# Graph attention on one core: how many pairs of gathers GpSimd keeps in flight (three or two)

## The reference

```
xn = layernorm(h)
q, k, v = xn @ wq + bq, xn @ wk + bk, xn @ wv + bv
scores = sum_d q[dst] * k[src] * scale
attn = softmax of scores over the edges (and the node itself) with the same dst
agg = segment_sum(attn * v[src], dst)
h = h + agg @ wo + bo;  h = h + gelu(layernorm(h) @ w1 + b1) @ w2 + b2
```

## Time and profile before

| | us |
|---|---|
| median of 3 timed runs | 4550.55 (4545.4 to 4551.32) |
| span of the profiled execution | 4968.2 |
| share of that span: PE, DVE, POOL, ACT busy | 76%, 74%, 66%, 45% |
| gathers (L1042): count, busy | 1760, 1775.7 |

### The profile page before, as it was taken

The page is one execution under the profiler, slowest core; times in us unless marked ns, Lnnn a source line. Parts: engine busy times, 40 slices in busy tenths (PEclk is TensorE's granted clock), DMA queues, the critical chain, the costliest instruction groups (busy, mean ns, idle before and its releaser), DMA issues. The chain is left out here.

```text
span 4968.2 us, 83663 instructions
## 1 busy us (share of the span) xinstructions
PE 3781.3 (76%) x17490; PEld 2898.5 (58%) x17491; DVE 3674.6 (74%) x10004; ACT 2245.8 (45%) x5559; POOL 3293.4 (66%) x2856
## 2 busy tenths in 40 slices
PE   2686677777777776999986677777777776888879
PEld 1344455555555555888853455555555555777766
DVE  5686688888888886666656688888888886666658
ACT  0122455555555553444410455555555563343323
POOL 2266666666666654888877666666666663888866
PEclk9698799988988998999998799999899997999989
DMA  4577666666666655777766666666666654777767
GB/s 107 176 173 172 195 184 180 184 181 180 185 175 184 178 159 127 152 160 153 160 133 132 199 181 187 183 181 181 180 180 181 183 172 97 148 143 148 143 157 222
DMA packets 683884, 831.82 MB, mean 167 GB/s; under 512 B 147301, under 2 KB 524321, under 8 KB 683589
## 3 DMA queue, kind: packets, MB, share of 16 engines
q0 software_dynamic: 261248, 480.06, 40.8%
q1 hardware_dynamic: 389483, 320.59, 22.4%
q10 hardware_dynamic: 32860, 28.05, 1.9%
HBM read 753.81 MB, written 124.16 MB: 177 GB/s over the span
## 5 line engine op out<-in xcount | busy, mean ns | idle before, releaser
L1042 POOL DMA_INDIRECT kv<-kv_scratch,src_u x1760 | 1775.7, 1009 | 955.1 <-issue 532.4
L1308 PE MATMUL sum_p<-msg,hot_s 128*128 128x273 f32 x3520 | 1132.7, 460 | 578.9 <-DVE sums L1174 452.6
L1308 PEld LDWEIGHTS sum_p<-msg,hot_s 128*128 128x128 f32 x3520 | 705.2, 215 | 893.1 <-DVE sums L1174 442.8
L1523 POOL DMA_INDIRECT sum_scratch<-ysum,dest x600 | 951.8, 1586 | 196.8 <-issue 137.8
L1296 PE MATMUL qe<-sums,hot_q 128*128 x3520 | 910.0, 404 | 99.6 <-ACT hot_q L1064 85.7
L1296 PEld LDWEIGHTS qe<-sums,hot_q 128*128 128x128 f32 x3520 | 719.5, 208 | 244.7 <-issue 115.7
L1174 DVE SCALAR_TENSOR_TENSOR sums<-sums,keep,sum_p 128x273 f32 x880 | 433.7, 493 | 463.9 <-remote 402.1
L1073 ACT ACTIVATE hot_s<-iota_f,ndrel_u 128x128 f32<-128x128 f32 x1760 | 558.7, 391 | 223.1 <-remote 173.2
L1148 DVE TENSOR_TENSOR prod<-qe,kv 128x1024 f32<-128x1024 f32 x440 | 535.6, 1217 | 64.2 <-DMA kv<-kv_scratch,src_u 35.0
L1163 DVE TENSOR_TENSOR msg<-kv,turned 128x1024 f32<-128x1024 f32 x440 | 532.6, 1210 | 7.5 <-issue 7.5
L1155 DVE TENSOR_REDUCE S<-prod 128x32 f32<-128x1024 f32 x440 | 533.8, 1213 | 0.6
(11 more groups left out here) (267 smaller groups left out, 5147.8 us busy)
## 6 DMA issues: line engine op xcount, KB each, us to landing
drow<-drel_scratch SPq DMA_DIRECT2D x220, 256.0 KB
kv<-kv_scratch,src_u POOLq DMA_INDIRECT x1760
ea<-in_edge_attr SPq DMA_DIRECT2D x52, 512.0 KB
srow<-in_src_rows SPq DMA_DIRECT2D x52, 512.0 KB
kv_scratch<-res SPq DMA_DIRECT2D x100, 256.0 KB
ea<-in_edge_attr SPq DMA_DIRECT2D x52, 384.0 KB
srow<-in_src_rows SPq DMA_DIRECT2D x52, 384.0 KB
h_scratch<-res SPq DMA_DIRECT2D x150, 128.0 KB
```

The lines of the kernel that those rows point to most:

```text
L1042: g.indirect_dma_start(out=kv[:, slot, :], out_offset=None, in_=KVd, in_offset=bass.IndirectOffsetOnAxis(ap=src_u[:, par, u:u + 1], axis=0 ...
L1308: ins = pe.matmul(sum_p[i][:, 0:XW], hot_s[:, q % 2, 2 * i + u, :], msg[:, q % 2, 2 * i + u, :], start=(u == 0), stop=(u == 1))
L1523: g.indirect_dma_start(out=sum_d[r], out_offset=bass.IndirectOffsetOnAxis(ap=dest[:, k, j:j + 1], axis=0), in_=ysum[:, k, j, :], in_offset ...
```

## The change

One constant changes. In both branches of the wait above, the pair whose landing is awaited is now j-2 in place of j-3 (counted back over the block's edge).

```diff
 HELD = 2
 PE_AT = GB - 2
-FLIGHT = 3
+FLIGHT = 2
 DVE_AT = 2
 RING = 3
```

## The result

| | us |
|---|---|
| before, median of 4 | 4549.89 (4545.4 to 4551.32) |
| changed, median of 4 | 5006.59 (5004.05 to 5016.31) |
| ratio | 1.1013, 95% interval 1.1000 to 1.1027 |

The change makes the kernel 457 us (10.1%) slower. The forecast was 4870 with a range to 4990: direction and place were right, and the loss was nearly half as large again as forecast (457 in place of 318).

What follows compares the result with a forecast made beforehand. The prediction took GpSimd's gather issue to bound the timed attention block at 21.1 us. 110 blocks x 3.1 us more, less a cover of 23, is 318 us on 4550.55: 4870 us, range 4560 to 4990.

Steps and rivals of the forecast that it cites:

- The bound and the timed block (21.1 us): In both attentions GpSimd's issue, 16 gathers at 1.31 us or 21.0 us, bounds a timed block of 21.1 us.
- its halts: GpSimd stops about 2.3 us twice a block, waiting for `sum_s`; taken to belong to the profiled execution, 310.7 us in all.
- r = 0.85 and L = 5.2: r: release to start of the waiting gather, 0.85 us; L: start of a pair's first gather to the pair's landing, 5.2.
- "The spacing of pairs is at least (L + r) / k": GpSimd's pair starts with k pairs in flight, never under 2.62 us; at FLIGHT = 2 3.02 us, 24.2 a block.
- The cover of 23 us: Gathers run 11.5 us ahead of their use; that lead is spent once in each attention, saving 23 us.
- FLIGHT = 3 "costs nothing": In the kernel before, spacing by landing is 2.02 us, below the floor of 2.62, so the wait costs nothing.
- Hidden by a short landing (1): With fewer gathers outstanding L falls to 4.4 us or less and the wait costs nothing: 4550 us; chance 0.07.
- the lone pair: A pair alone on the DMA engines, begun at 4089.75, last bytes before 4093.50: L at least about 3.7 us.
- Halts real (2): Timed blocks also take about 24.9 us, so 24.2 fits inside: 4550 to 4605 us; chance 0.11.
- Smaller L + r (3): L + r is 0.4 to 0.6 us smaller than taken: 4600 to 4740 us; chance 0.15.
- Faster (4): Fewer gathers share the DMA engines with `drow` and masks, so one-hot matrices come earlier: 4528 us; chance 0.05.
- the four loaded rows: Products that waited for landings at the attention's start bound L from above: 7.2, 5.9, 5.0 and 5.8 us.

Runs made afterwards that it cites:

- the shortened attention: Kernel before (FLIGHT = 3) with the first attention stopped after 37 of its 55 blocks, all else in full: 4169.3 us, ratio 0.9157.
- two gathers fewer: Kernel before (FLIGHT = 3) with the second gather of pairs 3 and 7 left out, 14 gathers a block in place of 16: 4493.9 us, ratio 0.9873.
- the run with small broadcasts: Changed kernel (FLIGHT = 2) loading only 8 of 1024 destination numbers each time after the first block: 4927.7 us, ratio 1.0832.
- the three runs with a spacing near the floor: A landing wait between a pair's two gathers, 4694.9 us; a semaphore for each gather with four gathers in flight, 4742.4; the same with three, 5152.3.

## Why the prediction came out as it did

**The bound and the timed block (21.1 us): right.** The forecast denied the trace its halts on the strength of 417.7 us. The runs bear it out: the shortened attention (21.3 us), two traces of other executions (21.06 with four pairs in flight, 21.07 with three), and two gathers fewer that give 0.5 us a block. What caused the halts in that one execution is open; that they belong to it and not to the kernel is shown. (In the rows, 525.10 is the last gather of block 1 and not the first of block 2; the 24.9 us a block stay.)

**r = 0.85 and L = 5.2: right**, as means. In the changed trace's landing events, over the 880 pairs, the last landing less the start of the pair's first gather averages 5.24 us, and a pair that waited starts 0.85 after the release (median). One pair in flight gives 5.1 + 0.85.

**"The spacing of pairs is at least (L + r) / k": the step that failed, by being used as an equality.** Taken with the average L it gave 24.2 us a block; measured are 25.3. The term was mis-sized by 1.1 us, 121 us in all. The spacing is the greater of the floor (2.62) and what each single landing allows, so late landings cost and early ones give nothing back. I replayed the rule start(j) = max(start(j-1) + 2.62, landed(j-2) + 0.85) with landing times in place of their mean. With all of them at the mean it gives 24.4 us a block, with the mean of each of the eight positions 24.9, with the actual series 25.3, and with the series shuffled 25.3; measured 25.3. So 0.2 us of the 1.1 is rounding and a mean of 5.24 in place of 5.2, and 0.9 is the unevenness (standard deviation 0.68 us), about half of it by position: pairs 1 and 5 land after 5.9 and 5.6 us, the others after 4.9 to 5.3. For pair 1 the run with small broadcasts shows what delays it; for pair 5 this is open. The replay is an argument from the trace; on the chip it is borne out by k = 1, where no floor interferes and the average does hold (42 to 48.7 expected, 47.6 measured), against the three runs with a spacing near the floor (4695, 4742 and 5152 us), all above the range by the average.

**The cover of 23 us: wrong, it was not there.** The lead of 11.5 us before the product belonged to the halts of that execution. The second trace of FLIGHT = 3 has pair 1's start 5.5 us before its product, which is its landing and little more; by the landing events a block's first product starts 0.6 us after the landing on average in its first attention and 0.8 in the second, and 0.2 in the changed kernel. So there is about half a microsecond to spend, not 11.5. GpSimd was the bound, so its gathers had no stock ahead. I applied the correction for the profiled execution to the block's length and forgot it for the lead.

The three terms close the sum: 318 + 121 + 23 = 462 = 110 x 4.2, against 457 measured.

**FLIGHT = 3 "costs nothing": nearly.** (5.2 + 0.85) / 3 = 2.02 is far below 2.62, yet four pairs in flight were 0.32% faster. Only a landing later than 3 x 2.62 - 0.85 = 7.0 us would stop the queue at three. There are such landings: 22 of the 736 pairs in the shortened trace, and the starts that waited for one cost 6 us there, about half of the 15 when counted for all 110 blocks. With four in flight no start waits. The other half is open.

**The rivals.** Hidden by a short landing (1): the lone pair near the end had misled; one in flight lands in 5.1 in the loop, not in 3.7. The rule of the Trainium skill, page "DMA: Bandwidth & Descriptors", section "Anatomy of one DMA — SWDGE (gpsimd) path", gave an estimate of 2.6 us for a gather; the medians are 3.5 (one pair in flight) to 4.0 here, 3.7 in the changed kernel, and 2.1 is the least. Those rows decide against it for gathers of this kind. Halts real (2): fell. Smaller L + r (3): fell. Faster (4): fell. The range ended 17 us too low. Its upper end allowed 4.2 us a block, just what was measured, but by a mean L of 5.5; the unevenness, which took up that room, was in none of its bounds, though the four loaded rows, 5.0 to 7.2, showed it. What put the time outside was the cover: without the 23 us the same 4.2 us a block end at 5012.

## What to carry to other kernels

With k transfers in flight, compare each landing and not the mean with k times the issue spacing: a wait for the k-th last needs (k x spacing - restart) above the slow landings, not the average one. Let transfers go one by one and not in pairs: with at most four gathers in flight either way, that gave back 58% of the loss here. And when the span is 9% above the timed runs, correct every quantity that leans on it, the leads and slacks too, or take a second trace from a neighbour of the kernel first.

## What the runs showed of the hardware that was not expected

- One execution of the kernel before showed halts that ended on the same semaphore (`sum_s`) for three engines, some 2.3 us for GpSimd twice a block, in a span 417.7 us above the timed runs; no wait for `remote` is in any other profiled execution here. Near 1037 the last matmul that raises the semaphore is recorded to end at 1032.25 and the semaphore's event comes at 1036.98; why is open.
- The mean time to landing of a pair depends little on how many pairs are in flight: 5.1 us with one, 5.2 with two, 5.6 with three, 5.5 with four. What rises is the throughput: 179 GB/s at two pairs, 215 at three and at four.
- Two broadcasts of 256 KB a block on another queue delay pair 1 of the block by some 0.7 us, and cost 79 us in all with two pairs in flight, and 5 us (0.1%) with three.
